# The low parts of the retention's queries: made by GpSimd behind its squares, not by VectorE

## The reference

```
q, k, v = proj(Wq), proj(Wk), proj(Wv)
q = _apply_rope(q, cos, sin)
k = _apply_rope(k, cos, sin)
qk = jnp.einsum('bhtd,bhsd->bhts', q, k) * (1.0 / np.sqrt(DH))
qk = qk * decay[None]
out = jnp.einsum('bhts,bhsd->bhtd', qk, v)
...
out = (out - mu) * jax.lax.rsqrt(var + EPS)
out = out * gn_weight.reshape(H, DH) + gn_bias.reshape(H, DH)
...
return jnp.einsum('btc,oc->bto', out, Wo)
```

## Time and profile before

| | us |
|---|---|
| median of 3 runs | 2248.8 (2246.24 to 2252.46) |
| span of the profiled execution (first to last instruction) | 2235.7 |
| TensorE busy | 2087.0 (93%) |
| VectorE busy | 1024.8 (46%) |
| ScalarE busy | 952.4 (43%) |
| GpSimd busy | 788.5 (35%) |
| mean granted TensorE clock | 0.977 |

### The profile page before, as it was taken

How to read it: one execution, slowest core, us unless ns; L and a number is a source line. 1 busy time by engine, 2 the same in 40 slices (tenths; PEclk the granted TensorE clock), 3 DMA queues, 4 the chain that set the end, 5 groups by cost and what they waited for, 6 DMA issues and landing times.

```text
span 2235.7 us, 36685 instructions
## 1 busy us (share of the span) xinstructions
PE 2087.0 (93%) x12648; PEld 1926.7 (86%) x12648; DVE 1024.8 (46%) x1683; ACT 952.4 (43%) x1663; POOL 788.5 (35%) x637
## 2 busy tenths in 40 slices
PE   4899999999789897899999999899999999999997
PEld 4788888888677776888888888799999999999987
DVE  7566676666663584366666666555200003000032
ACT  2356565556652443356655555522222224111141
POOL 0434333333556445134433323332222323222244
PEclk9999999999889998999999999899999999999999
DMA  5465655545411122556555554211111111211123
GB/s 171 133 162 151 161 139 145 149 134 147 118 41 34 30 75 74 168 149 166 155 148 138 158 141 120 82 58 65 57 60 62 59 63 57 65 57 57 65 75 96
DMA packets 140378, 233.86 MB, mean 105 GB/s; under 512 B 49240, under 2 KB 93528, under 8 KB 140184
## 3 DMA queue, kind: packets, MB, share of 16 engines
q1 hardware_dynamic: 140312, 232.99, 36.1%
HBM read 174.12 MB, written 55.53 MB: 103 GB/s over the span
## 4 chain that ended last, share of the span: by engine, by line
PE 76%; DVE 8%; ACT 4%; POOL 4%; issue 3%; DMA 3%; SPq 1%; DVEq 0%; POOLq 0%; ACTq 0%
PE psS L340 14%; PE psS L342 14%; PE psS L341 14%; PE psO L1849 5%; PE psJ L340 4%; PE psJ L341 3%; PE psJ L342 3%; PE psS L1808 3%; PE psT L340 2%; PE psT L1835 2%; PE psT L341 2%; PE psT L342 2%; PE psS L1835 2%; DVE psS L1282 1%; PE psO L340 1%
## 5 line engine op out<-in xcount | busy, mean ns | idle before, releaser
L761 POOL TENSOR_TENSOR fw_lo<-raw,fw_hi 128x1024 fp32r<-128x1024 f32 x96 | 235.2, 2450 | 540.7 <-ACT fw_hi L1067 540.6
L340 PE MATMUL psS<-hid_hi,fw_hi 128*128 128x400 f32 x1152 | 397.8, 345 | 3.5 <-DVE hid_lo L1731 2.9
L342 PE MATMUL psS<-hid_hi,fw_lo 128*128 128x400 f32 x1152 | 398.6, 346 | 0.0
L341 PE MATMUL psS<-hid_lo,fw_hi 128*128 128x400 f32 x1152 | 398.2, 346 | 0.0
L578 POOL TENSOR_TENSOR pT<-p,pT 128x600 fp32r<-128x600 f32 x128 | 188.8, 1475 | 529.3 <-ACT pT L860 527.9
L1282 DVE TENSOR_REDUCE psS<-psS 100x1 f32<-100x722 f32 x256 | 234.7, 917 | 152.4 <-PE psS L1808 152.0
L1731 DVE TENSOR_TENSOR hid_lo<-h_act,hid_hi 128x800 fp32r<-128x800 f32 x32 | 40.8, 1341 | 528.1 <-ACT hid_hi L1178 528.1
L340 PEld LDWEIGHTS psS<-hid_hi,fw_hi 128*128 128x128 f32 x1152 | 216.9, 188 | 7.3 <-DVE hid_lo L1731 5.1
L342 PEld LDWEIGHTS psS<-hid_hi,fw_lo 128*128 128x128 f32 x1152 | 218.2, 189 | 0.0
L340 PE MATMUL psJ<-cT_hi,wk_hi 128*128 128x362 f32 (+1 forms) x512 | 182.0, 356 | 37.8 <-DVE cT_lo L1276 15.4
L341 PEld LDWEIGHTS psS<-hid_lo,fw_hi 128*128 128x128 f32 x1152 | 216.9, 188 | 0.0
(11 more groups left out here) (340 smaller groups left out, 4448.1 us busy)
## 6 DMA issues: line engine op xcount, KB each, us to landing
kS<-k_parts SPq DMA_DIRECT2D x384, 180.5 KB
raw<-ffn_dram SPq DMA_DIRECT2D x96, 512.0 KB, 3.6
k_parts<-kst SPq DMA_DIRECT2D x64, 362.0 KB, 3.3
k_parts<-kst SPq DMA_DIRECT2D x64, 360.0 KB, 3.0
ctx_raw<-ctxT_dram SPq DMA_DIRECT2D x32, 361.0 KB, 3.9
qS<-q_parts SPq DMA_DIRECT2D x192, 50.0 KB, 2.6
q_parts<-qst SPq DMA_DIRECT2D x16, 400.0 KB, 2.5
ctx_late<-ctxT_dram SPq DMA_DIRECT2D x14, 362.0 KB, 4.7
```

The source lines that it names most:

```text
L340: nc.tensor.matmul(out, st[0], mv_[0], start=first, stop=False)
L341: nc.tensor.matmul(out, st[0], mv_[1], start=False, stop=False)
L342: return nc.tensor.matmul(out, st[1], mv_[0], start=False, stop=last)
L761: nc.gpsimd.tensor_tensor(fw.lo[:, e, :], raw[:, e, :], fw.hi[:, e, :], ALU.subtract)\
```

## The change

The instruction that makes qs.lo moves from VectorE's program to GpSimd's. In the batches it stands on GpSimd right behind the squares of batch b - 1, ahead of geps; for batch 0 it stands ahead of keys_lo(0). The semaphores are the same ones (R.q_hi before, R.q_low after).

```diff
+            def queries_part_lo(b):
+                wait_apart(pool, R.q_hi, b + 1)
+                nc.gpsimd.tensor_tensor(qs.lo[:, :, :], qk[0][:, :, bass.ds(b * T, T)], qs.hi[:, :, :], ALU.subtract)\
+                  .then_inc(R.q_low, 1)
+
             def retention_pool(b, prev=True, before=True, after=True):
                 if prev:
                     wait_apart(pool, R.g_dev, b)
                     nc.gpsimd.tensor_tensor(gsq[:, :], gd[:, :], gd[:, :], ALU.mult).then_inc(R.g_sq, 1)
+                if after:
+                    queries_part_lo(b + 1)
+                if prev:
                     wait_apart(pool, R.g_sum2, b)
...
+            queries_part_lo(0)
             keys_lo(0)
             retention_pool(0, prev=False, before=False)
...
-            def queries_part_lo(b):
-                ts = bass.ds(b * T, T)
-                dve.wait_ge(R.q_hi, b + 1)
-                nc.vector.tensor_tensor(qs.lo[:, :, :], qk[0][:, :, ts], qs.hi[:, :, :], ALU.subtract).then_inc(R.q_low, 1)
-
...
                 if cur:
                     decayed(0)
                     decayed(1)
-                if after:
-                    queries_part_lo(b + 1)
                 if cur:
                     p_lo(0)
...
-            queries_part_lo(0)
             retention_values_lo(0)
```

## The result

The changed kernel takes 2263.74 us in the median of nine runs (2260.23 to 2266.79), the kernel before 2248.8 in its nine: ratio 1.0075, 95% interval 1.0052 to 1.0098, which is 12 to 22 us. The medians differ by 14.9 us. A second session gave 1.0054 (1.0029 to 1.0079) for the same kernel, with medians 15.4 us apart. The forecast was 2258.3 and +0.42%, range 2253.5 to 2263.5.

What follows compares the result with a forecast made beforehand. The prediction took the chain of waits around the retention as the bound, repeating every 13.43 us in steady batches. Its terms 6.6 + 2.1 + 0.8 = 9.5 us, set on the 2248.8 median, gave 2258.3 us, range 2253.5 to 2263.5.

Steps and rivals of the forecast that it cites:

- Part (1): Retention's start: batch 0's qs.lo waits on GpSimd behind both ro splits, so scores(0) start later; +6.6 us.
- Part (2): Batch 0: TensorE idles 8.4 us, so scores(0) start at 1.2 GHz; +2.1 us, bounds -0.3 and 7.5.
- rival (b): Retention: low clock lasts all of batch 0 and more; +14.9 us, 2263.7 us; chance 0.12.
- rival (a): Retention: clock does not fall (2255.9 us), or the lock does not bite (2256.3); both together 2253.9; chance 0.20.
- the lock: Steady batches: GpSimd's qs.lo holds VectorE's first low part, both using SBUF; 0.15 us later per batch.
- Part (3): Batches 1 to 6: GpSimd's qs.lo holds VectorE's first low part of the probabilities; +0.8 us over six batches.
- The covers: Steady batches: later query transfers cost nothing, with 1.2 us of cover before scores; geps and the q_hi wait also free.
- rival (d): Each batch: query transfers become the bound, SyncE slipping beyond 1.2 us of cover; about +12.5 us, 2261.3 us; chance 0.08.
- (c): Behind the retention: the late start is absorbed by a stage bounded by something that does not move; 2247.4 us; chance 0.05.

Runs made afterwards that it cites:

- start_only: Kernel before with only batch 0's queries_part_lo moved to GpSimd, behind the ro splits, the other seven left on VectorE; ratio 1.0084.
- batches_only: Changed kernel with batch 0's queries_part_lo kept on VectorE, so only batches 1 to 7 moved to GpSimd; ratio 1.002.
- before_ro: Changed kernel with batch 0's queries_part_lo on GpSimd ahead of the two ro splits instead of behind them; ratio to the kernel before 1.0031.
- before_gaps: Kernel before with 3 filler products on TensorE behind the output projection of each batch from 1 on; median 2239.96 us, ratio 0.9976.

## Why the prediction was wrong

The direction was right, the measured time lies 0.2 us outside the range, and the 14.9 us between the medians is half as much again as the 9.5 forecast.

**Part (1), the first batch, +6.6 us: right.** From the first xb_hi copy to scores(0) it was 8.91 us and is 15.51, +6.60 us, to the hundredth. start_only has it with all other batches on VectorE, batches_only is without it, and before_ro, which moves nothing but this call in front of the splits, brings it down to 0.5.

**Part (2), "TensorE's clock, +2.1 us": the step that failed.** For the place it was meant for it was nearly right: scores(0) to scores(1) is 11.67 us (754.44 to 766.11) for 9.96, +1.7. The forecast then let the clock be as before in everything behind batch 0, and put that at nothing. By the medians the clock term is 14.9 us less the 7.4 of parts (1) and (3), so 7.5 and not 2.1; by the mean clocks of all executions on record it is 8.5. Single traces have more: the three of the changed kernel lose 18.0, 21.0 and 27.4 us on the yardstick, of which 10.6, 13.6 and 20.0 are left beside the waits, but they are held against quick executions of before, which overstates it. The trace behind the forecast is one of these: it shows the batches at 1.00, and I took it for typical and its distance from the median for time around the span. Of the twelve altered kernels all but before_gaps have a yardstick 8 us or more above those traces. Why longer waits in the retention go with a lower clock in the next attention, and at which places, stays open.

Two numbers are near the result by chance. The bound of 7.5 for this part was worked out for batch 0 running slow throughout, and rival (b), which goes with it, names 14.9 us and 2263.7, the measured difference and median. But its mechanism is not what was found: in the first trace the granted clock is back at 1.00 from 760 us on, batch 0 costs 1.7 us, and the rest is lost in later batches or in the next attention. Of rival (a), neither half came: the clock fell in front of scores(0) in all three traces, and the lock did bite.

**Part (3), the steady batches, +0.8 us: right.** The period is 13.57 us for 13.43; the held low part takes 0.90 us (0.57 before) and ends 0.44 us behind GpSimd, 0.45 forecast. In the first trace, whose batches 1 to 7 were at full clock, they sum to +0.7: 81.14 us from batch 1's first p_raw to batch 7's, for 80.45. The Trainium skill's rule ("SBUF — State Buffer", section "Who interferes with whom"), that the second of the two is blocked to the end of the first, agrees in kind; its letter would have made 0.28 a batch, and the row of the earlier meeting was the better measure (0.14). The fourth low part, in the last section, does not follow it.

**The covers.** TensorE's steady scores never waited for transfers (in the first trace of the changed kernel all its waits from 766 to 853 us, 6.5 us, are for VectorE's pb.lo): rival (d) did not come. Nor did (c): nothing behind the retention gave the late start back.

## What to carry to other kernels

Moving an operation to an idle engine moves it behind everything that engine's program has ahead of it; look at its first instance, before the loop, more closely than at the steady ones. Where TensorE is almost but not quite busy, the time of a small change is its own waits plus a term for the clock that can be as large, and part of it can lie in stages the change never touches. Set the traced execution's own time against the median before taking the trace for typical; compare traces stage by stage with the granted clock beside each; and compare the times of executions at equal mean clock, which here separated the waits (7.6 us) from the clock (8.5 us) without any further trace. Products that nothing depends on, put into short waits, show what the clock's share is.

## What was unexpected

The kernel before, unaltered, scatters by some 25 us (2236 to 2262), and nine tenths of the variance go along with its mean granted clock. A wait of 2.27 us in front of scores(0) was enough for the clock to be down behind it in before_ro, where 1.76 us was not in the kernel before. And in each steady batch of the changed kernel the fourth low part of the probabilities takes 1.94 us (802.45) for 0.57, although it starts 0.48 us before GpSimd's kb.lo (802.93 to 803.95); it ends 0.44 us behind it, like one that was blocked by it. With nearly the same distances (788.66 and 789.15 in the kernel before) it takes 0.57 us in all traces of before and in the steady batches of start_only that run at full clock. It goes with the moved batches, in batches_only as well. It is not on the chain, since VectorE's next work waits for r_oT.hi, but TensorE waits 0.56 us for it. Why the one that starts first is the one that waits stayed open, as did the places at which the clock falls in the next attention.
